# Reordering the opening of a fused cross-attention and expert kernel: first query by parts, one row normalisation on another engine, statistics of later pairs moved

## The reference, cut to what matters

```python
x = x + xattn(_layernorm(x), ctx)       # 16 sequences x 128 rows x 256
x = x + ffn(_layernorm(x))

def xattn(h, memory):                   # h is the layer-normed x
    normed = h * rsqrt(mean(h*h) + 1e-6) * norm_w
    v_pool = concat([normed, memory], axis=1)
    q = einsum('bsh,oh->bso', normed, q_w)
    k = einsum('bth,oh->bto', v_pool, k_w)
    logits = q @ k.T / sqrt(256)        # causal over the 128 rows, open over memory
    h_tilde = softmax(logits) @ v_pool
    alpha = sigmoid(h @ gate_w.T + gate_b)
    return (1 - alpha) * h + alpha * h_tilde

def ffn(rows):                          # 8 experts, 512 rows each, gathered by top_idx
    g = gelu(rows[tok_e] @ W1[e] + b1[e])
    out_e = g @ W2[e] + b2[e]
    out[tok_e] += out_e * combine_weights[tok_e, e]
```

## Time and profile before

| what | value |
|---|---|
| median of three runs | 274.86 us (274.32 to 274.9) |
| profiled execution | 275.01 us, span 273.2 us |
| TensorE busy | 263.7 us, 97% |
| VectorE busy | 218.4 us, 80% |
| ScalarE busy | 188.2 us, 69% |
| GpSimd busy | 156.9 us, 57% |
| mean granted clock of TensorE | 0.996 |

### The profile page before, as it was taken

The page is one execution under the profiler, slowest core; times in us unless marked ns, Lnnn a source line. Parts: engine busy times, 40 slices in busy tenths (PEclk is TensorE's granted clock), DMA queues, the critical chain, the costliest instruction groups (busy, mean ns, idle before and its releaser), DMA issues.

```text
span 273.2 us, 5127 instructions
## 1 busy us (share of the span) xinstructions
PE 263.7 (97%) x1477; PEld 225.8 (83%) x1477; DVE 218.4 (80%) x553; ACT 188.2 (69%) x349; POOL 156.9 (57%) x152
## 2 busy tenths in 40 slices
PE   7899999999989999999999999999999999999993
PEld 3688899999876888888888888888888888888983
DVE  1899999899985779968878896796887889689453
ACT  2687899887666975786676587668657758773540
POOL 4349765565768717656456466655645656514525
PEclk9999999999999999999999999999999999999998
DMA  5986257588446945454464544645446561210211
GB/s 154 341 232 199 94 154 200 148 231 270 133 149 150 388 154 157 129 169 155 134 208 154 156 142 135 168 118 207 160 138 180 160 181 56 59 35 34 65 49 69
DMA packets 30560, 42.44 MB, mean 155 GB/s; under 512 B 5521, under 2 KB 24283, under 8 KB 30416
## 3 DMA queue, kind: packets, MB, share of 16 engines
q1 hardware_dynamic: 25120, 29.74, 35.0%
q0 software_dynamic: 4608, 12.24, 15.4%
q10 hardware_dynamic: 816, 0.26, 0.4%
HBM read 33.54 MB, written 9.24 MB: 157 GB/s over the span
## 4 chain that ended last, share of the span: by engine, by line
PE 81%; DVE 6%; issue 4%; DMA 4%; POOL 1%; ACT 1%; SPq 0%; DVEq 0%; POOLq 0%
PE bank L1423 19%; PE bank L1202 12%; PE bank L1203 12%; PE bank L1204 12%; PE bank L1424 10%; PE bank L1250 4%; PE bank L1294 3%; DMA x_all<-in_x_dram 2%; PE bank L1351 2%; DMA x_all<-token_rows,idx_all 2%; PE bank L1370 1%; PE bank L1371 1%; PE bank L1374 1%; PE bank L1318 1%; POOL out_dram L557 1%
## 5 line engine op out<-in xcount | busy, mean ns | idle before, releaser
L752 ACT ACTIVATE keysT<-bank,biasT 128x512 f32<-128x512 f32 x63 | 43.6, 692 | 55.6 <-PE bank L1204 39.3
L557 POOL DMA_INDIRECT out_dram<-h,sidx x32 | 36.7, 1146 | 40.2 <-DVE h L1094 34.8
L547 POOL DMA_INDIRECT x_all<-out_dram,idx_all x32 | 36.6, 1143 | 23.6 <-DMA out_dram<-h,sidx 16.0
L1202 PE MATMUL bank<-x_hi,w_parts 128*128 128x512 f32 (+1 forms) x114 | 45.1, 396 | 0.0
L1203 PE MATMUL bank<-x_lo,w_parts 128*128 128x512 f32 (+1 forms) x114 | 44.4, 389 | 0.0
L1204 PE MATMUL bank<-x_hi,w_parts 128*128 128x512 f32 (+1 forms) x114 | 44.1, 387 | 0.0
L1119 DVE TENSOR_TENSOR g_lo<-keysT,g_hi 128x512 fp32r<-128x512 f32 x32 | 22.1, 692 | 27.0 <-ACT g_hi L753 26.3
L543 POOL DMA_INDIRECT x_all<-token_rows,idx_all x28 | 30.7, 1095 | 18.9 <-DVE factor L1143 12.4
L1423 PE MATMUL bank<-w_parts,g_hi 128*128 128x512 f32 x112 | 40.5, 396 | 0.0
L1124 DVE TENSOR_TENSOR w_parts<-w_raw,w_parts 128x512 fp32r<-128x512 f32 x56 | 38.4, 686 | 0.0
L758 ACT CAST w_parts<-w_raw 128x512 fp32r<-128x512 f32 x56 | 34.9, 623 | 0.0
(11 more groups left out here) (187 smaller groups left out, 681.5 us busy)
## 6 DMA issues: line engine op xcount, KB each, us to landing
w_raw<-in_L_ffn_W_dram SPq DMA_DIRECT2D x32, 512.0 KB
idx_rows<-in_L_ffn_top_idx_dram SPq DMA_DIRECT2D x8, 256.0 KB, 4.1
out_dram<-x SPq DMA_DIRECT2D x8, 256.0 KB, 2.9
hn_cnat<-in_ctx_dram SPq DMA_DIRECT2D x7, 256.0 KB, 2.8
token_rows<-xn SPq DMA_DIRECT2D x7, 256.0 KB, 2.2
hn_cnat<-in_L_ffn_b_dram SPq DMA_DIRECT2D x1, 1024.0 KB
x_all<-in_x_dram SPq DMA_DIRECT2D x3, 256.0 KB, 6.8
x_all<-in_x_dram SPq DMA_DIRECT2D x1, 768.0 KB, 9.4
```

Source lines behind the costliest of these rows:

```text
L547: g.indirect_dma_start(accg[:, t, :], None, flat, list_of(e, t)).then_inc(acc_in[t], 16)
L557: g.indirect_dma_start(flat, idx(sidx[:, t:t + 1].bitcast(U32), 0), newrow[:, t, :], None, bounds_check=N - 1, oob_is_err=False).then_inc( ...
L752: a.activation(g32[:, f % NG, :], ps_up[f % 2][:, :], ACT.Gelu_apprx_tanh, bias=bias)
L1202: t_.matmul(dst, lhs_hi, rhs_hi, start=first, stop=False)
```

## The change

SyncE loads the first pair's context ahead of the second piece of x. On TensorE the first query is written out with the products of `hnT_hi` first in each half; then come the gate weight's transposes, and the spreading of `norm_w` and `gate_b` over the partitions is put behind them. ScalarE copies in the same new order, leaves the `hn` of pair one to VectorE, and takes `hnT_hi` of pair one out between its two exponentials. VectorE makes the low parts of M before it looks at the second piece of x, makes `gateT_lo` and `hn` of pair one ahead of the first masked maximum, does sequences 4 and 5 behind it and 6 to 9 after pair zero's gate logits; sequences 10 to 15 go to pair one. VectorE's pairs are written out instead of looped. GpSimd's powers and shifts follow: 4 and 5 before pair zero, 6 to 9 in pair zero, 10 and 11 in pair one, 12 to 15 in pair two.

```diff
             load_weight(0, q_w, wts_in)
+            load_ctx(0)
             load_x(1, 2, 4)
-            load_ctx(0)
...
             x_powers(2, 4, 2)
-            hn_shifts(2, 4, 2)
+            pool.wait_ge(bc_rdy, 1)
+            pool.wait_ge(hn_rdy, 4)
+            normed_rows(0, 0)
...
             hn_shifts(4, 6, 3)
-            pool.wait_ge(bc_rdy, 1)
-            normed_rows(0, 0)
-            x_powers(6, 10, 4)
-            hn_shifts(6, 10, 4)
...
                 if is_first(p):
-                    x_powers(10, NB, 5)
-                    hn_shifts(10, NB, 5)
+                    x_powers(6, 10, 4)
+                    hn_shifts(6, 10, 4)
...
                     rstd(p - 1, 1 - s)
+                if p == 1:
+                    x_powers(10, 12, 5)
+                    hn_shifts(10, 12, 5)
+                if p == 2:
+                    x_powers(12, NB, 6)
+                    for b in (12, 14):
+                        hn_shifts(b, b + 2, 6)
...
             def hn_rows(p, s):
-                if not (isinstance(p, int) and p == 1):
-                    act.wait_ge(n_rdy, p - 1)
+                act.wait_ge(n_rdy, p - 1)
                 act.wait_ge(hn_rdy, 2 * p)
-                act.wait_ge(hs_rdy, p if isinstance(p, int) else 4)
+                act.wait_ge(hs_rdy, p - 1 if isinstance(p, int) else p - 2)
...
                                  accum_out=rsum[:, b:b + 1]).then_inc(exp_rdy, 1)
+                    if is_first(p) and b == 0:
+                        hn_transposed(1, 1)
                 if is_first(p):
-                    hn_transposed(1, 1)
...
             normed_transposed(0, 0)
+            query(0)
+            act.wait_ge(setup_mm, 3)
+            a.copy(gateT_hi[:, :, :], ps_gate).then_inc(setup_ev, 1)
...
             a.copy(vec_bc[:, :], banks[7][:, :]).then_inc(bc_rdy, 1)
-            query(0)
-            hn_rows(1, 1)
-            act.wait_ge(setup_mm, 3)
-            a.copy(gateT_hi[:, :, :], ps_gate).then_inc(setup_ev, 1)
...
                 dve.wait_ge(x_steps, steps[0])
-                if b0:
+                if b0 > 2:
...
             hn_rows(0, 0)
-            x_sums(2, 3, 1)
...
             hnT_low(0, 0)
-            x_sums(3, 4, 1)
+            x_sums(2, 4, 1)
...
             x_variances(2, 4)
-            x_stats(4, 6, 2)
-            x_variances(4, 6)
-            h_rows(0, 0, False)
-            x_rms(0, 4, 2)
-            x_sums(6, 8, 3)
+            x_sums(4, 6, 2)
...
                     dve.wait_ge(pT_mm, p)
+                else:
+                    gateT_low()
+                    dve.wait_ge(pow_rdy, 2)
+                    hn_rows(1, 1)
                 for b in range(2):
-                    if is_first(p) and b == 1:
-                        gateT_low()
...
                 else:
+                    x_aggregates(4, 6)
+                    x_variances(4, 6)
+                    h_rows(0, 0, False)
+                    hnT_low(1, 1)
+                    x_rms(0, 4, 2)
...
                     v.tensor_copy(idx_f[:, :], idx_all[:, :, :].rearrange("p t e -> p (t e)")).then_inc(idx_rdy, 1)
-                    x_sums(8, 10, 3)
-                    hnT_low(1, 1)
-                if isinstance(p, int) and p == X_GROUPS[-1][0] // 2:
-                    x_rms(10, NB, 5)
                 dve.wait_ge(gate_mm, p + 1)
-                if isinstance(p, int):
-                    dve.wait_ge(x_steps, steps[0])
+                dve.wait_ge(x_steps, steps[0])
...
                 if is_first(p):
-                    x_aggregates(6, 10)
+                    x_stats(6, 10, 3)
...
                     h_rows(1, 1, False)
-                    x_stats(10, NB, 4)
...
                     stats2(p - 1, 1 - s)
+                if p == 1:
+                    aggr2(p - 1, 1 - s)
+                    x_stats(10, NB, 4)
+                    x_variances(10, 12)
+                    x_variances(12, NB)
+                    x_rms(4, 10, 4)
...
                     hnT_low(p + 2, s)
-                if is_first(p):
-                    x_variances(10, NB)
-                else:
+                if p > 1:
                     aggr2(p - 1, 1 - s)
-                    if not is_last(p):
-                        h_rows(p + 1, 1 - s)
+                if p == LAST - 3:
+                    x_rms(10, NB, 6)
+                if not is_first(p) and not is_last(p):
+                    dve.wait_ge(pow_rdy, min(p + 2, 6))
+                    h_rows(p + 1, 1 - s)
...
                         .then_inc(late_lo_rdy, 1)
-                if is_first(p):
-                    x_rms(4, 10, 4)
-                    dve.wait_ge(x_steps, steps[0])
-                elif not is_last(p):
+                if not is_first(p) and not is_last(p):
                     shift(p - 1, 1 - s)
-                    dve.wait_ge(pow_rdy, 5)
-
-            each_pair(dve, attention)
+
+            for p in range(NPAIR):
+                attention(p, p % 2, p // 2)
...
             hn_transposes(0, 0)
+            context_transposes(0, 0, 0)
+            pe.wait_ge(setup_lo, 2)
+            pe.wait_ge(hnT_hi_rdy, 1)
+            for m in range(KH):
+                c = slice(m * P, (m + 1) * P)
+                for k in range(KH):
+                    t_.matmul(ps_q[:, m, :], M_hi[:, k, c], hnT_hi[:, 0, k, :], start=(k == 0), stop=False)
+                    t_.matmul(ps_q[:, m, :], M_lo[:, k, c], hnT_hi[:, 0, k, :], start=False, stop=False)
+                pe.wait_ge(hnT_lo_rdy, 1)
+                for k in range(KH):
+                    last = t_.matmul(ps_q[:, m, :], M_hi[:, k, c], hnT_lo[:, 0, k, :], start=False, stop=(k == KH - 1))
+            last.then_inc(q_mm, 1)
+            pe.wait_ge(gatew_in, 16)
+            for k in range(KH):
+                for o in range(KH):
+                    last = t_.transpose(ps_gate[:, k, o * P:(o + 1) * P], wts[:, 2, o, k * P:(k + 1) * P], ident[:, :])
+            last.then_inc(setup_mm, 1)
...
             last.then_inc(bc_mm, 1)
-            context_transposes(0, 0, 0)
-            pe.wait_ge(setup_lo, 2)
-            query(0, 0)
-            pe.wait_ge(gatew_in, 16)
-            for k in range(KH):
-                for o in range(KH):
-                    last = t_.transpose(ps_gate[:, k, o * P:(o + 1) * P], wts[:, 2, o, k * P:(k + 1) * P], ident[:, :])
-            last.then_inc(setup_mm, 1)
```

## The result

| | before | after |
|---|---|---|
| median, us | 274.88 | 278.06 |
| runs, us | 274.32, 274.86, 274.9, 275.0 | 276.75, 277.99, 278.12, 278.72 |
| granted TensorE clock, mean of the run | 0.996 (profiled execution) | 0.999, 0.992, 0.992, 0.993 |
| profiled execution (its span), us | 275.01 (273.2) | 277.99 (276.2) |

The kernel before has one run more here than in the median of 274.86 that the forecast started from. The change made the kernel slower: the ratio is 1.0112, with the interval [1.0093, 1.0132]. The forecast was 276.8, between 275.0 and 278.4. The time is 1.3 us above the forecast, and of the four runs the one at 276.75 is the one whose clock did not fall.

What follows compares the result with a forecast made beforehand. TensorE was taken as the bound, with under 0.1 us slack at pair two's softmax. VectorE's terms summed to +2.0 us there, +1.9 on TensorE; 275.01 + 1.9 = 276.9, forecast as 276.8 at the median, range 275.0 to 278.4.

Steps and rivals of the forecast that it cites:

- the forecast's own case: Pair two's second masked maximum on VectorE comes +1.0 to +2.6 us later, giving 275.9 to 277.4 us; 55%.
- the cascade: Rival, pair zero: VectorE's rms stands behind x_plus_h and a cast behind normed, leaving 0.1 us of the gain; 278.1, 20%.
- the clock: Rival: TensorE's clock falls to 1.2 GHz after its wait of nearly 3 us, adding 1 to 1.5 us; 278.1, 4%.
- The place: One TensorE wait of 2 to 3 us before pair two's transposes of the probabilities, on ScalarE's exponential.
- The opening: Logits at about 11.85 instead of 12.88, pair two's keysT at about 18.3; the microsecond is down to 0.1 us.
- VectorE up to pair one's maximum: Less work between pair two's hnT_lo and pair one's masked maximum: VectorE gains -1.3 us (-1.6 to -0.1).
- Added work: Moved statistics and rms in pair one, ahead of pair two's softmax: +3.4 us on VectorE (3.0 to 3.6).
- The collisions: VectorE beside GpSimd: pair zero's residual no longer meets x_plus_h, -1.0 us; var_eps is held by w_lo, +0.6 (0 to 1.0).
- One-hot: VectorE reaches the one-hot a little before ScalarE's list is written and waits: +0.5 us (0 to 0.9).
- the shift's -0.2: The shift of pair zero's x2 no longer has to be waited for: -0.2 us.
- TensorE keeps its gain: Rival: pair two's second maximum ends by about 33.0, so TensorE keeps what it won; 274.1 us, 12%.
- the sides cancel: Rival: all bounds fall to the good, the terms come to 0.0 and the time is 274.9; 9%.

Runs made afterwards that it cites:

- the products: The changed kernel with TensorE's pairs written out and eight matmuls on unread junk data ahead of pair two's wait for the exponentials: 276.93 us, 1.0087 against the kernel before.

## Why the prediction was right, and where it was off

*The number.* 278.06 lies inside the stated range, but above the forecast's own case of 275.9 to 277.4. It is inside because the range was drawn out for the cascade and for the clock. Of the 3.20 us that TensorE lost at pair two, 1.69 are the mechanism of the forecast and 1.51 are the clock, which had been given 4%. That the range held owes as much to luck as to the sum.

*The place.* The loss of time was forecast at one spot, TensorE's wait for pair two's exponential. It is there, 2.01 us (2 to 3 expected). One wait was forecast and there are two: the added work stands ahead of pair two's hnT_lo as well, and TensorE waits 0.51 us for that at 33.38. The statistics alone bring the long one (2.02), and putting them back takes it away from pair two, with one of 1.77 us in pair one in its place. That the later pairs keep their pace is shown by the product of pair seven, 3.13 late where pair two's is 3.20.

*The opening.* Logits at 11.85 forecast, 11.76 measured; keysT 18.3, 18.24; the 0.1 us that is left, 0.16. The opening alone leaves nothing at all. By the spread between executions the microsecond itself was nearer to 0.7.

*VectorE up to pair one's maximum.* -1.3 forecast, -1.05 measured. Between rinv and the diffs there is a gap of 0.55 us in the row at 23.13 that the walk did not have; which wait it is stays open.

*Added work.* +3.4 forecast. The rows give 29.19 to 32.55: 3.36.

*The collisions.* Residual -1.0, measured -1.03. var_eps +0.6: it took 0.92 instead of 0.47, +0.45.

*One-hot.* +0.5 (0 to 0.9) forecast for a wait on ScalarE's list. It did not wait: its row at 24.73 is 0.49 us long and has no wait before it. That is the term that failed in the sum, by 0.5. The measured terms with the shift's -0.2 add to -1.05 + 3.36 - 1.03 + 0.45 - 0.2 = +1.53; the second maximum came 1.73 later. The 0.2 us between them is in a row that the walk did not have: the two aggregates behind pair zero's bn_stats, which now follow these directly, take 0.41 us (the row at 27.91). Before, with hnT_lo between, they took 0.23:

```profile
30.55 0.23 DVE L906 BATCH_NORM_AGGREGATE mv<-bn6b 128x2 f32<-128x6 f32 x2
```

TensorE's +1.9 came to +1.69.

*The cascade in pair zero, 20%.* Half of it came. The cast idx_f met x_plus_h, but nothing stood behind normed. VectorE and GpSimd after the change:

```profile
16.70 1.28 DVE L950 CAST idx_f<-idx_all 128x32 f32<-128x32 int32 x1
...
16.62 1.32 POOL L502 TENSOR_TENSOR x_plus_h<-x_all,h 128x512 f32<-128x512 f32 x1
```

The rms had slipped in at 16.36 and 16.55, as held against this rival. The stall of 1.1 us did not show at pair one's maximum, as VectorE waited for keysT behind it.

*The clock, 4%.* This was mis-sized, in chance and not in price. It came in three of the four runs, the profiled one among them. The measured +1.51 us is the upper end of the forecast's +1 to +1.5, and its 278.1 is the median of 278.06. The forecast itself put a stand of nearly 3 us on the path and called it "longer than any after the start"; no row of before spoke for so small a chance. 276.8 is right for the runs in which the clock held (276.75 here, 276.93 with the products, 276.06 with the pairs written out, 276.74 and 277.44 with the statistics alone).

*TensorE keeps its gain, or the sides cancel.* Neither came here. Yet in the kernel with casts and wait moved, the microsecond is kept in just the way described, because VectorE's second maximum of pair two starts at 31.18, below the 33.0 at which that rival was to decide.

*What the parts are worth.* Alone: opening +0.2%, hn +0.4%, GpSimd's order none, statistics with their powers +1.3%. They add up to more than the 1.1% of the whole. The likely reason, argued and not shown, is that they delay the same join: what one gives up stands partly in another's wait.

## What to carry to other kernels

Before work is moved off a late place, look for the next point at which the same engine is waited for, and count its slack there: here VectorE had 0.87 us free in ten, and 3.4 us were put in front of a join with 0.1 us of slack. 1.7 us of it came out there, and not all, only because VectorE had won 1.05 us up to pair one's maximum and 1.03 us at the residual. Work won in front of such a join is lost again in the first wait; what paid was taking single stalls off the engine that sets the join, two casts and a wait put where they cost nothing, -0.4% together with GpSimd's order and the written-out pairs. And when a forecast has the matrix engine stand for 2 us in its middle, price the clock with it.

## What the runs showed of the hardware

A wait of 2.0 us of TensorE, with one of 0.5 us a microsecond ahead of it, brought its granted clock to 0.50, 1.2 GHz, for about 3.3 us after it, and cost 1.5 us. By the mean clock of each run it did so in eight of the ten runs of the kernel after and of its copy with TensorE's pairs written out (clock 0.992 to 0.994, 277.94 to 278.72), and not in two (0.999; 276.75 and 276.06). With the statistics moved alone, where the same two waits stand, it did so in three of five. With products on idle data in the wait it did so in none of five, and a wait of 1.77 us in pair one (statistics back) did so in none of six. Nor is such a fall wholly new: of 57 further runs of the kernel before, one has 0.990 and 277.19 us.

Even instructions of VectorE on a few elements stood until GpSimd's 128x512 instruction ended, where both worked in SBUF: idx_f 1.28 us, tok_f 0.86 and 1.09, var_eps 0.92, beside 0.16 to 0.18 alone. A one-hot of 512 columns took 1.19 instead of 0.49. The Trainium skill's page "SBUF — State Buffer", section "SBUF: two separate sides", describes such a lock, and all of these rows agree. Not every instruction stood, and the time of one beside GpSimd has to be read from its row: in the kernel after, the two gate products that start at 17.89 (0.86 us, one input from a bank) and the four bn_stats behind them (1.39 us) ran beside GpSimd's normed of 17.89 to 19.16 at their usual length. So did two aggregates at 14.28 (0.24 us) beside its normed of 13.74 to 15.03, while the neg_mean right behind them stood until that ended (0.50 instead of 0.17).
